# The loads of A and B move from SyncE's queue to ScalarE's, behind its copies of z

## The chip, the cores and the metric

The kernel runs on one core of a Trainium2 chip. The metric is the device time of one execution in microseconds. SyncE (SP) issues DMAs and waits; TensorE (PE), VectorE (DVE), ScalarE (ACT) and GpSimd (POOL) compute. ScalarE can issue DMAs too, on a queue of its own.

## The reference

For each of 64 batches `x[b]` (128 channels by 2048 times, f32) goes through two residual steps. The first picks one of 16 matrices of 128 x 128 by an id, the second one of 64 low rank adapters (A and B, rank 16) by another id:

```python
W = weights[itok_B_0_15]
x = x + jnp.einsum('bct,bcd->bdt', x, W)
Bx = jnp.einsum('bni,bri->bnr', x, B[itok_B_4_50])
x = x + jnp.einsum('bnr,bor->bno', Bx, A[itok_B_4_50])   # scaling 1
```

Each x is read once and each output written once, 1 MB (2^20 bytes) a batch each way. A and B of a batch lie side by side in one row of `lora`, 256 KB, which one DMA brings into `ab_in`.

## The kernel before

Two batches are a round, two kinds of round alternate, and two rounds (four batches, `BODY`) are a turn. Turn 0 and the last turn are written out, the 14 between them are a hardware loop on every engine. Buffers `x_in`, `x_out`, `ab_in`, `at`, `z_all`, `m_sel` have four copies each, one for each batch of a turn. PSUM's eight banks (`bank`) hold 512 columns each.

What happens to one batch:

- SyncE loads x (`load_x`, L128) and A with B (`load_ab`, L131). The id of the adapter is read from SBUF into a register (`value_load`, L125).
- GpSimd makes `m_sel`, the chosen matrix plus the identity (L209).
- TensorE mixes x by `m_sel` in four units of 512 columns (`mix_units`, L388). Each unit fills a bank. A round has only three banks for its eight units (`F_BANKS`), so from the fourth unit on TensorE waits until ScalarE has copied the unit three before it.
- ScalarE copies each unit from its bank to `ft` (`copy_units`, L256).
- TensorE multiplies `ft` by B (`sum_z`, L404) into a z bank, in four parts of 16 rows. ScalarE and VectorE copy two parts each out of it (`take_z`, L263 and L312).
- GpSimd adds the four parts in three additions (L218, L223) into the first 16 rows of `z_all`. ScalarE copies these rows to three other places (`place_z`, L268).
- VectorE transposes A (L328, semaphore `a_turned`). One round later TensorE multiplies it by z (`add_low_rank`, L428), and VectorE adds `ft` to it and writes `x_out` (L319). SyncE stores it (`store`, L149).

Each engine carries out its own list in the order written. In a round, TensorE mixes both batches, sums z of both, and then does the low rank product of the two batches of the round before. ScalarE copies eight units, takes z of both batches, places z of both. SyncE stores the two batches of a turn ago, loads two x as soon as the slots are free (`f_made`), and then loads A and B for the batches four further on. That last step (`next_ab`) waits until z of the slot's batch is made and A is transposed, since both read `ab_in`.

Instructions of VectorE, ScalarE and GpSimd are handed to the engine by its sequencer, which also does the register reads and arithmetic, the branches and the issuing of DMAs, in the order of the program.

Of the kernel before, what the change touches and what calls it, by code (L numbers as in the profile page):

```python
# [10 lines left out]
BATCHES, CHANNELS, TIME = 64, 128, 2048  # L11
# [15 lines left out]
ROUND = 2  # L27
BODY = 2 * ROUND
# [16 lines left out]
def live(count):  # L45

    return not (isinstance(count, int) and count <= 0)


def begun(b):  # L50

    return not (isinstance(b, int) and b < 0)


def f_bank_of(kind, k, u, final):

    return LAST_F[u] if final and k == ROUND - 1 else F_BANKS[kind][(UNITS * k + u) % len(F_BANKS[kind])]


def cond_lora_residual(nc, x, both_ids, weights, lora, out):  # L60
    with ExitStack() as ctx:
        def sbuf(name, shape, dtype=F32):
            return ctx.enter_context(nc.sbuf_tensor(name, shape, dtype))
# [4 lines left out]
        def sem(name):  # L68
            return ctx.enter_context(nc.semaphore(name))
# [3 lines left out]
        ids = sbuf("ids", [1, 2, BATCHES], I32)  # L73
# [6 lines left out]
        ab_in = [sbuf(f"ab_in{k}", [P, (JS + CHUNKS) * RANK]) for k in range(BODY)]  # L80
# [9 lines left out]
        ids_in = sem("ids_in")  # L90
# [3 lines left out]
        ab_loaded = [sem(f"ab_loaded{k}") for k in range(BODY)]  # L94
# [5 lines left out]
        a_turned = sem("a_turned")  # L100
# [3 lines left out]
        z_done = sem("z_done")  # L104
# [9 lines left out]
        def rows_of_unit(u):  # L114
            return slice(BLOCK * u, BLOCK * u + RANK)

        def rows_of_z(z_bank, c):
            return bank[z_bank][TILE * c:TILE * c + RANK, 0:P]
# [3 lines left out]
        @block.sync  # L122
        def _(sp):
            def adapter_of(b):
                return sp.value_load(ids[0:1, 1, bass.ds(b, 1)], min_val=0, max_val=lora.shape[0] - 1)  # L125

            def load_x(k, b):
                sp.dma_start(x_in[k][:], x[b]).then_inc(x_loaded[k], 16)  # L128

            def load_ab(k, adapter):  # L130
                sp.dma_start(ab_in[k][:], lora[adapter]).then_inc(ab_loaded[k], 16)  # L131

            sp.dma_start(ids[:].rearrange("p n b -> p (n b)"), both_ids).then_inc(ids_in, 16)  # L133
            sp.dma_start(w_all[:], weights).then_inc(w_in, 16)  # L134
            for i in range(2):
                cols = slice(TIME // 2 * i, TIME // 2 * (i + 1))
                sp.dma_start(x_in[0][:, cols], x[0, :, cols]).then_inc(first_loaded[i], 16)
            load_x(1, 1)
            sp.wait_ge(ids_in, 16)
            for k in range(ROUND):  # L140
                load_ab(k, adapter_of(k))
            for k in range(ROUND, BODY):
                load_x(k, k)
            for k in range(ROUND, BODY):
                load_ab(k, adapter_of(k))

            def store(k, b):
                sp.wait_ge(added, UNITS * (b + 1))
                sp.dma_start(out[b], x_out[k][:]).then_inc(stored[k], 16)  # L149

            def next_x(k, b):
                sp.wait_ge(f_made, UNITS * (b - BODY + 1))
                load_x(k, b)

            def next_ab(k, b):
                adapter = adapter_of(b)
                sp.wait_ge(z_done, b - BODY + 1)
                sp.wait_ge(a_turned, b - BODY + 1)
                load_ab(k, adapter)


            def turn(q, last):
                for kind in range(KINDS):
                    b = BODY * q + ROUND * kind
                    slots = range(ROUND * kind, ROUND * (kind + 1))
                    if begun(b - BODY):
                        for i, k in enumerate(slots):
                            store(k, b - BODY + i)
                    if not last:
                        for i, k in enumerate(slots):  # L170
                            next_x(k, b + BODY + i)
                        for i, k in enumerate(slots):
                            next_ab(k, b + BODY + i)

            turn(0, False)
            with sp.Fori(1, TURNS - 1) as q:
                turn(q, False)
            turn(TURNS - 1, True)

            def store_part(b, units):  # L180
                cols = slice(UNIT * units[0], UNIT * (units[-1] + 1))
                sp.dma_start(out[b, :, cols], x_out[b % BODY][:, cols]).then_inc(stored[b % BODY], 16)

            for k in range(BODY - 2):
                store(k, BATCHES - BODY + k)
            for units in ((0, 1), (2, 3)):
                sp.wait_ge(added, UNITS * (BATCHES - 2) + units[1] + 1)
                store_part(BATCHES - 2, units)
            sp.wait_ge(evacuated, 2)
            store_part(BATCHES - 1, (1, 2))  # L190
            sp.wait_ge(added, UNITS * (BATCHES - 1) + 1)
            store_part(BATCHES - 1, (0,))
            for k in range(BODY - 2):
                sp.wait_ge(stored[k], 16 * TURNS)
            sp.wait_ge(stored[BODY - 2], 16 * (TURNS - 1 + 2))
            sp.wait_ge(stored[BODY - 1], 16 * (TURNS - 1 + 3))
# [51 lines left out]
        @block.scalar  # L248
        def _(act):
            def copy_units(kind, i, b, final):  # L250
                k = ROUND * kind + i
                for u in range(UNITS):
                    if live(UNITS * (b - BODY) + u + 1):
                        act.wait_ge(added, UNITS * (b - BODY) + u + 1)
                    act.wait_ge(f_made, UNITS * b + u + 1)
                    nc.scalar.copy(ft[k][u][:], bank[f_bank_of(kind, i, u, final)][:]).then_inc(copied, 1)  # L256

            def take_z(i, b, z_bank):
                act.wait_ge(z_done, b + 1)
                if live(b - 1):  # L260
                    act.wait_ge(z_paired, 2 * (b - 1))
                for c in (0, 2):
                    nc.scalar.copy(z_part[i][c][:], rows_of_z(z_bank, c)).then_inc(z_taken_act, 1)  # L263

            def place_z(k, b):
                act.wait_ge(z_summed, b + 1)
                for u in range(1, UNITS):
                    nc.scalar.copy(z_all[k][rows_of_unit(u), :], z_all[k][rows_of_unit(0), :]).then_inc(z_placed, 1)  # L268

            def normal_round(kind, b):  # L270
                for i in range(ROUND):
                    copy_units(kind, i, b + i, False)
                for i in range(ROUND):
                    take_z(i, b + i, Z_BANKS[i])
                for i in range(ROUND):
                    place_z(ROUND * kind + i, b + i)

            def turn(q):
                for kind in range(KINDS):
                    normal_round(kind, BODY * q + ROUND * kind)  # L280

            turn(0)
            with act.Fori(1, TURNS - 1) as q:
                turn(q)
            normal_round(0, BATCHES - BODY)
            b = BATCHES - 2
            copy_units(1, 0, b, True)
            take_z(0, b, Z_BANKS[0])
            place_z(BODY - 2, b)
            b = BATCHES - 1  # L290
            copy_units(1, 1, b, True)
            take_z(1, b, Z_BANKS[0])
            act.wait_ge(z_summed, BATCHES)
            for u in BY_ACT:
                nc.scalar.copy(z_all[BODY - 1][rows_of_unit(u), :], z_all[BODY - 1][rows_of_unit(BY_DVE[0]), :]  # L295
                               ).then_inc(z_placed, 1)
            act.wait_ge(stored[BODY - 1], 16 * (TURNS - 1))
            act.wait_ge(low_done, BATCHES)
            for u in range(1, UNITS):
                nc.scalar.copy(x_out[BODY - 1][:, UNIT * u:UNIT * (u + 1)], bank[LAST_OWN[u]][:]).then_inc(evacuated, 1)  # L300
            act.wait_ge(evacuated, UNITS - 1)
            cols = slice(UNIT * (UNITS - 1), TIME)
            act.dma_start(out[BATCHES - 1, :, cols], x_out[BODY - 1][:, cols]).then_inc(stored[BODY - 1], 16)
# [200 lines left out]
```

## Time and profile before

| | |
|---|---|
| median of 3 runs | 393.79 us (390.11 to 395.64) |
| the profiled execution | 395.34 us, its span 393.5 us |
| granted TensorE clock, mean | 0.982 of full |
| busy: PE, PE weight loads, DVE, ACT, POOL | 376.5, 354.3, 230.8, 238.4, 112.2 us |
| DMA queue of SyncE | 151.79 MB, 96.1% of the 16 engines' span |
| issues: x, stores, A with B | x63, x62 of 1 MB, x64 of 256 KB (and the parts of the first x and the last stores) |

Times in rows are us from the start of the span, except where they say ns. The span goes from the first to the last instruction, and the execution's own time lies 1.8 us above it. Busy time of an engine doesn't count what its sequencer does: register reads, waits, branches and the issue of DMAs. Rows of a sequencer have a q behind the engine (SPq, ACTq). An f32 matmul shows as two records. In brackets stands the idle time of the engine before the row and who ended it.

### The profile page before, as it was taken

To read this page: it belongs to the slowest core of one execution; us is meant where nothing else is said; L and a number is where in the kernel's file an instruction comes from. 1 tells how busy PE (TensorE), PEld (TensorE's weight loads), DVE (VectorE), ACT (ScalarE), POOL (GpSimd) and SP (SyncE) were. 2 spreads that over 40 slices of the span, in tenths; PEclk is the share of its full clock that TensorE was granted. 3 is DMA by queue.
4 is the path that set the end of the run, shared out by engine and by line. 5 is a ranking of instruction groups with operands and counts; after the bars stand their busy time and mean duration, and the time that the engine had idled before them with its cause. 6 is when DMAs were issued, how large, how long until landed. Compare 5 with 4: busy or idle time off the path is not lost.

```text
span 393.5 us, 16869 instructions
## 1 busy us (share of the span) xinstructions
PE 376.5 (96%) x6170; PEld 354.3 (90%) x6170; DVE 230.8 (59%) x447; ACT 238.4 (61%) x579; POOL 112.2 (29%) x260
## 2 busy tenths in 40 slices
PE   7989989999999999999999999999999999999981
PEld 7979979999999999999999999999999999999871
DVE  0226762676555667755566775556677555667763
ACT  1566644666656666665666666566666666666541
POOL 2122330333332223333222333322233332223210
PEclk9999988999999999999999999999999999999996
DMA  7999997999999999999999999999999999999567
GB/s 272 417 362 347 407 409 277 345 415 386 406 414 412 408 416 415 415 404 414 404 418 410 416 405 410 414 405 409 414 415 414 410 406 406 415 403 413 223 250 277
DMA packets 28383, 152.24 MB, mean 387 GB/s; under 512 B 3153, under 2 KB 3154, under 8 KB 12242
## 3 DMA queue, kind: packets, MB, share of 16 engines
q1 hardware_dynamic: 28226, 151.79, 96.1%
q10 hardware_dynamic: 144, 0.26, 0.2%
q8 instruction: 9, 0.15, 0.1%
q14 instruction: 4, 0.03, 0.0%
HBM read 84.94 MB, written 67.11 MB: 386 GB/s over the span
## 4 chain that ended last, share of the span: by engine, by line
PE 93%; DMA 2%; issue 2%; ACT 1%; DVE 1%; POOL 1%; SPq 0%; POOLq 0%; DVEq 0%; ACTq 0%
PE bank L388 60%; PE bank L428 16%; PE bank L404 16%; DMA x_in<-in_x 2%; POOL z_pair L218 0%; ACT x_out L300 0%; DVE x_out L319 0%; ACT z_all L268 0%; POOL z_all L223 0%; ACT ft L256 0%; DVE z_pair L335 0%; DVE z_part L312 0%; DVE z_all L339 0%; SPq L134 0%; SPq L133 0%
## 5 line engine op out<-in xcount | busy, mean ns | idle before, releaser
L388 PE MATMUL bank<-m_sel,x_in 128*128 128x128 f32 x2048 | 240.8, 279 | 2.9 <-ACT ft L256 1.7
L388 PEld LDWEIGHTS bank<-m_sel,x_in 128*128 128x128 f32 x2048 | 234.1, 194 | 8.6 <-DVE x_out L319 2.7
L256 ACT COPY ft<-bank 128x512 f32<-128x512 f32 x256 | 146.1, 587 | 65.5 <-PE bank L388 63.5
L319 DVE TENSOR_TENSOR x_out<-bank,ft 128x512 f32<-128x512 f32 x253 | 154.3, 681 | 19.6 <-PE bank L428 19.5
L218 POOL TENSOR_TENSOR z_pair<-z_part 16x128 f32<-16x128 f32 x126 | 54.2, 446 | 217.0 <-DVE z_part L312 198.6
L312 DVE COPY z_part<-bank 16x128 f32<-16x128 f32 x126 | 36.2, 287 | 121.2 <-PE bank L404 119.2
L268 ACT COPY z_all<-z_all 16x128 f32<-16x128 f32 x189 | 56.0, 296 | 46.9 <-POOL z_all L223 43.8
L428 PE MATMUL bank<-z_all,at 16*128 16x128 f32 x2048 | 70.0, 282 | 2.8 <-issue 1.8
L428 PEld LDWEIGHTS bank<-z_all,at 16*128 16x128 f32 x2048 | 63.2, 187 | 10.1 <-issue 10.0
L404 PE MATMUL bank<-ft,ab_in 128*16 128x128 f32 x2048 | 65.6, 274 | 1.6 <-issue 1.6
L404 PEld LDWEIGHTS bank<-ft,ab_in 128*16 128x16 f32 x2048 | 51.4, 96 | 10.6 <-issue 5.1
L263 ACT COPY z_part<-bank 16x128 f32<-16x128 f32 x128 | 32.9, 257 | 33.2 <-PE bank L404 31.6
L328 DVE STREAM_TRANSPOSE at<-ab_in 128x512 f32<-128x512 f32 x64 | 41.5, 684 | 14.5 <-DMA ab_in<-in_lora 14.5
L209 POOL TENSOR_TENSOR m_sel<-w_all,ident 128x128 f32<-128x128 f32 x64 | 29.2, 457 | 38.9 <-PE bank L388 23.4
L223 POOL TENSOR_TENSOR z_all<-z_pair 16x128 f32<-16x128 f32 x63 | 28.1, 446 | 7.3 <-POOL z_pair L218 4.5
L436 PE MATMUL bank<-ident 128*128 128x128 f32 x26 | 5.9, 427 | 1.6 <-POOL ident L202 1.6
L436 PEld LDWEIGHTS bank<-ident 128*128 128x128 f32 x26 | 5.6, 331 | 1.6 <-POOL ident L202 1.6
L300 ACT COPY x_out<-bank 128x512 f32<-128x512 f32 x3 | 1.6, 594 | 1.5 <-PE bank L428 1.5
L256 ACT ACT_TABLE_LOAD x1 | 1.3, 1283 | 0.8 <-PEq L489 0.8
L295 ACT COPY z_all<-z_all 16x128 f32<-16x128 f32 x2 | 0.6, 295 | 0.8 <-DVE z_all L339 0.8
L335 DVE TENSOR_TENSOR z_pair<-bank,z_part 16x128 f32<-16x128 f32 x2 | 0.6, 287 | 0.8 <-ACT z_part L263 0.7
L339 DVE TENSOR_TENSOR z_all<-z_pair 16x128 f32<-16x128 f32 x2 | 0.6, 280 | 0.1
(7 smaller groups left out, 0.9 us busy)
## 6 DMA issues: line engine op xcount, KB each, us to landing
x_in<-in_x SPq DMA_DIRECT2D x63, 1024.0 KB, 11.3
out<-x_out SPq DMA_DIRECT2D x62, 1024.0 KB, 10.1
ab_in<-in_lora SPq DMA_DIRECT2D x64, 256.0 KB, 10.0
out<-x_out SPq DMA_DIRECT2D x3, 512.0 KB, 4.3
w_all<-in_weights SPq DMA_DIRECT2D x1, 1024.0 KB, 4.9
x_in<-in_x SPq DMA_DIRECT2D x2, 512.0 KB, 6.9
out<-x_out SPq DMA_DIRECT2D x1, 256.0 KB, 4.6
out<-x_out ACTq DMA_DIRECT2D x1, 256.0 KB, 5.9
```

What stands on the lines that cost most here:

```text
L209: nc.gpsimd.tensor_tensor(m_sel[k][:], w_all[:, cond, :], ident[:], ALU.add).then_inc(m_picked, 1)
L218: nc.gpsimd.tensor_tensor(z_pair[i][:], parts[2 * i][:], parts[2 * i + 1][:], ALU.add).then_inc(z_paired, 1)
L223: nc.gpsimd.tensor_tensor(z_all[k][rows_of_unit(0), :], z_pair[0][:], z_pair[1][:], ALU.add).then_inc(z_summed, 1)
L256: nc.scalar.copy(ft[k][u][:], bank[f_bank_of(kind, i, u, final)][:]).then_inc(copied, 1)
L263: nc.scalar.copy(z_part[i][c][:], rows_of_z(z_bank, c)).then_inc(z_taken_act, 1)
L268: nc.scalar.copy(z_all[k][rows_of_unit(u), :], z_all[k][rows_of_unit(0), :]).then_inc(z_placed, 1)
L312: nc.vector.tensor_copy(z_part[i][c][:], rows_of_z(z_bank, c)).then_inc(z_taken_dve, 1)
L319: nc.vector.tensor_tensor(x_out[k][:, UNIT * u:UNIT * (u + 1)], bank[banks[u]][:], ft[k][u][:], ALU.add).then_inc(added, 1)
L328: nc.vector.transpose(at[k][:], blocks).then_inc(a_turned, 1)
L388: last = nc.tensor.matmul(to[:, P * c:P * (c + 1)], x_in[k][:, UNIT * u + P * c:UNIT * u + P * (c + 1)], m_sel[k][:], start=(c == 0), stop ...
L404: last = nc.tensor.matmul(rows_of_z(z_bank, c), ab_in[k][:, first:first + RANK], ft[k][u][:, P * c:P * (c + 1)], start=(u == 0), stop=(u = ...
L428: last = nc.tensor.matmul(bank[banks[u]][:, P * c:P * (c + 1)], at[k][rows, js, :].rearrange("r j i -> r (j i)"), z_all[k][rows, :], start ...
```

## The change

SyncE's `next_ab` goes. ScalarE gets one of its own: it reads the adapter's id into a register, waits for `a_turned`, and issues the load. It runs in each normal round but the last, between the second `take_z` and the first `place_z`. The wait for `z_done` isn't repeated, for `take_z` has just waited for the same. The loads of the first four batches stay with SyncE. The semaphores that tell of a landed load are the same.

```diff
--- before.py
+++ after.py
@@ -152,12 +152,6 @@
                 sp.wait_ge(f_made, UNITS * (b - BODY + 1))
                 load_x(k, b)
 
-            def next_ab(k, b):
-                adapter = adapter_of(b)
-                sp.wait_ge(z_done, b - BODY + 1)
-                sp.wait_ge(a_turned, b - BODY + 1)
-                load_ab(k, adapter)
-
 
             def turn(q, last):
                 for kind in range(KINDS):
@@ -169,8 +163,6 @@
                     if not last:
                         for i, k in enumerate(slots):
                             next_x(k, b + BODY + i)
-                        for i, k in enumerate(slots):
-                            next_ab(k, b + BODY + i)
 
             turn(0, False)
             with sp.Fori(1, TURNS - 1) as q:
@@ -267,11 +259,19 @@
                 for u in range(1, UNITS):
                     nc.scalar.copy(z_all[k][rows_of_unit(u), :], z_all[k][rows_of_unit(0), :]).then_inc(z_placed, 1)
 
-            def normal_round(kind, b):
+            def next_ab(k, b):
+                adapter = act.value_load(ids[0:1, 1, bass.ds(b, 1)], min_val=0, max_val=lora.shape[0] - 1)
+                act.wait_ge(a_turned, b - BODY + 1)
+                act.dma_start(ab_in[k][:], lora[adapter]).then_inc(ab_loaded[k], 16)
+
+            def normal_round(kind, b, last=False):
                 for i in range(ROUND):
                     copy_units(kind, i, b + i, False)
                 for i in range(ROUND):
                     take_z(i, b + i, Z_BANKS[i])
+                if not last:
+                    for i in range(ROUND):
+                        next_ab(ROUND * kind + i, b + BODY + i)
                 for i in range(ROUND):
                     place_z(ROUND * kind + i, b + i)
 
@@ -279,10 +279,11 @@
                 for kind in range(KINDS):
                     normal_round(kind, BODY * q + ROUND * kind)
 
+            act.wait_ge(ids_in, 16)
             turn(0)
             with act.Fori(1, TURNS - 1) as q:
                 turn(q)
-            normal_round(0, BATCHES - BODY)
+            normal_round(0, BATCHES - BODY, last=True)
             b = BATCHES - 2
             copy_units(1, 0, b, True)
             take_z(0, b, Z_BANKS[0])
```

## Rows read from the trace of the kernel before

**Rows 1.** The page: busy times, the queue, the chain that ended last.

```profile
PE 376.5 (96%) x6170; PEld 354.3 (90%) x6170; DVE 230.8 (59%) x447; ACT 238.4 (61%) x579; POOL 112.2 (29%) x260
...
q1 hardware_dynamic: 28226, 151.79, 96.1%
...
PE 93%; DMA 2%; issue 2%; ACT 1%; DVE 1%; POOL 1%; SPq 0%; POOLq 0%; DVEq 0%; ACTq 0%
```

**Rows 2.** Timeline, even round: start us, us, engine, line, operation, tiles, count, idle before.

```profile
205.73 1.73 SPq L131 DMA_DIRECT2D ab_in<-in_lora  x2
...
206.09 0.54 ACT L263 COPY z_part<-bank 16x128 f32<-16x128 f32 x2 [0.48 <-PE bank L404]
...
207.96 7.41 PE L388 MATMUL bank<-m_sel,x_in 128*128 128x128 f32 x64
...
209.93 1.60 ACT L256 COPY ft<-bank 128x512 f32<-128x512 f32 x3
...
211.99 1.29 DVE L328 STREAM_TRANSPOSE at<-ab_in 128x512 f32<-128x512 f32 x2
```

**Rows 3.** Timeline, the next, odd round.

```profile
217.44 0.54 ACT L263 COPY z_part<-bank 16x128 f32<-16x128 f32 x2 [0.39 <-PE bank L404]
...
218.69 0.94 ACT L268 COPY z_all<-z_all 16x128 f32<-16x128 f32 x3 [0.72 <-POOL z_all L223]
...
219.41 5.85 PE L388 MATMUL bank<-m_sel,x_in 128*128 128x128 f32 x50
...
220.25 0.94 ACT L268 COPY z_all<-z_all 16x128 f32<-16x128 f32 x3 [0.62 <-POOL z_all L223]
...
221.22 1.76 ACT L256 COPY ft<-bank 128x512 f32<-128x512 f32 x3
```

**Rows 4.** Landing of the x loads (L128) issued in 80:100 and in 340:360.

```profile
DMA to landing us min/median/max: 7.7/7.7/7.8
...
DMA to landing us min/median/max: 17.2/17.6/17.8
```

**Rows 5.** Timeline of the last rounds.

```profile
368.31 3.65 PEld L388 LDWEIGHTS bank<-m_sel,x_in 128*128 128x128 f32 x32 [0.21 <-DMA x_in<-in_x]
...
372.90 0.81 PEld L404 LDWEIGHTS bank<-ft,ab_in 128*16 128x16 f32 x32 [0.94 <-issue]
```

**Rows 6.** Timeline of the first round.

```profile
21.55 1.56 ACT L256 COPY ft<-bank 128x512 f32<-128x512 f32 x3
22.19 1.97 PEld L388 LDWEIGHTS bank<-m_sel,x_in 128*128 128x128 f32 x17 [1.84 <-ACT ft L256]
```

**Rows 7.** Timeline, an early pair of ab issues on SyncE.

```profile
39.66 1.56 SPq L131 DMA_DIRECT2D ab_in<-in_lora  x2
```

**Rows 8.** The ab issues (L131), ns min/median/max.

```profile
L131 SPq DMA_DIRECT2D ab_in<-in_lora x64: 332/333/857, 4.2 to 355.8; - x64
```

**Rows 9.** Register reads, SyncE in 60:160 and 160:360, GpSimd in 60:240.

```profile
L125 SPq TENSOR_LOAD <-ids x17: 264/285/653, 67.1 to 158.8; - x17
...
L125 SPq TENSOR_LOAD <-ids x35: 262/545/794, 160.4 to 355.1; - x35
...
L208 POOLq TENSOR_LOAD <-ids x30: 283/290/413, 71.1 to 232.4; - x30
```

**Rows 10.** The one DMA that ScalarE issues (L303).

```profile
L303 ACTq DMA_DIRECT2D out<-x_out x1: 374/374/374, 387.1 to 387.1; - x1
```

**Rows 11.** The chain in order of time, 48 to 72 us.

```profile
52.94 1.76 issue
...
56.38 10.03 PE bank L388 x64
```

**Rows 12.** ScalarE's L261 between 216.9 and 217.7 us.

```profile
L261 ACTq ALU_OP  x1: 38/38/38, 217.4 to 217.4; - x1
```

**Rows 13.** Windows: us, busy us of each engine, granted clock, DMA share, GB/s.

```profile
55.20:61.90 6.70, 6.70 (x45) 6.48 (x41) 4.19 (x7) 1.46 (x4) 0.92 (x2) 0.50 0.96 393
...
370.00:386.00 16.00, 12.73 (x244) 11.27 (x242) 12.58 (x24) 7.53 (x20) 1.30 (x3) 1.00 0.68 275
```

## The prediction, made before the change was run

> **What bounds the kernel now.** I read the page first: TensorE is busy 96% of the span and the 16 DMA engines 96% too, ScalarE 61%, and the chain that ended last is 93% TensorE [rows 1]. So two resources are nearly full, and the first question is which one sets the pace. The timeline of two rounds answers it [rows 2, 3]. A round handles two batches. TensorE runs 64 records of the mix (L388), 64 of the z product (L404) and 64 of the low rank product (L428), one set behind the other. The mix starts at 207.96 and again at 219.41, so a round takes 11.45 us. TensorE sets the pace, and whatever holds it adds to the time.
>
> The DMA queue is the second limit, not yet in force. The loads of x issued around 90 us land 7.7 us after their issue, those around 350 us 17.6 us after it [rows 4]. The backlog thus grows by 9.9 us in 260 us, which are 22.7 rounds: 0.44 us a round. The transfers would need 11.9 us for the work of a round, against TensorE's 11.45. The four x buffers pay for it: only at 368.31 does the mix wait for x, for 0.21 us [rows 5], just before the end. The transfers cost nothing today.
>
> **ScalarE's order, and how late it already is.** In each round ScalarE copies eight banks to `ft`, takes z of both batches (L263), waits for GpSimd's sum, and places z of both (L268), 0.94 us each. Then come the copies of the next round. The mix holds three banks, so its fourth unit waits until the first unit was copied. Of the 64 matmul records of a round's mix, eight are one unit. They take 7.41 us, 0.116 each, so unit 3 starts 24 records, 2.78 us, behind the mix: at 210.74 in one round and at 222.19 in the next. The first copy of the round is done at 209.93 + 0.59 = 210.52 and 221.22 + 0.59 = 221.81 [rows 2, 3]. What TensorE needs between the end of a copy and its start shows in the first round, where it did wait: copy from 21.55 to 22.14, TensorE at 22.19, 0.05 us [rows 6]. So ScalarE is early by only 0.17 us in one kind of round and 0.33 us in the other. That is all the cover that anything put ahead of `place_z` has, beside ScalarE's own idle time there (0.72 and 0.62 us before the two placings, waiting for GpSimd).
>
> **The change, part by part.** *Removed from SyncE:* two reads of an adapter id, the wait for z and `a_turned`, and two issues a round. SyncE is on the chain with 0% [rows 1], so its time is free today and stays so. Worth 0.
>
> *Added to ScalarE's sequencer,* behind the second `take_z` and ahead of the first `place_z`: twice the register read of the id, its range check, the address arithmetic, the wait for `a_turned`, and the DMA issue. The wait is free: the transposes of these batches ran at 211.99 and are over at 213.28, before z at 217.44 [rows 2, 3]. The rest costs sequencer time, and ScalarE's copies can't be dispatched meanwhile, though ScalarE itself is idle. Its price is on SyncE today. From the start of one ab issue to the start of the next there lies one whole sequence. A pair takes 1.56 us in all at 39.66 [rows 7] and 1.73 us at 205.73 [rows 2]; less one issue of 0.33 us [rows 8] that is 1.23 and 1.40 us a sequence. The spread is the register read: 285 ns median from 60 to 160 us and 545 ns from 160 to 360 us on SyncE, 290 ns up to 240 us on GpSimd [rows 9]; it is long where the backlog is long. On ScalarE the wait for z drops out (an estimated 0.05 us), and the issue is 374 ns instead of 333, from the one that ScalarE has [rows 10]. So a sequence costs 1.22 us at the low end and 1.39 at the high end, two 2.44 and 2.78.
>
> *The path that follows.* Odd round: the last `take_z` starts at 217.44. Plus 2.44, plus 0.05 to the first dispatched copy (an estimate) is 219.93; GpSimd's sums were ready when the placings began, at 218.69 and 220.25 [rows 3], so the first placing doesn't wait for them any more and the second hardly. Six placing copies take 2 x 0.965 (220.25 to 221.22 is one set with its gaps): 221.86. First `ft` copy 0.59, signal 0.05: 222.50. TensorE wants it at 222.19, so it stalls 0.31 us. Even round: 206.09 + 2.49 + 1.93 + 0.64 = 211.15 against 210.74: 0.41 us. Mean 0.36 us; by the high price 0.34 more, 0.70 us. The later copies catch up, each 0.59 us against 0.89 us of a unit, so it is one stall a round. I take 0.42 us, near the low end, because a slower round of TensorE (11.87 us) lets the transfers nearly keep up (11.9), the backlog stays at the values of the first half, and with it the reads stay short.
>
> *How often.* 30 rounds issue loads (turns 0 to 14, two each). In the round that ends at 66 us the mix takes 10.03 us instead of 7.4 [rows 11], so its fourth unit comes late anyway: no stall there. In the first, where TensorE waits for the copy already [rows 6], the shift counts in full, 0.6. So 29 stalls: 29 x 0.42 = 12.2 us; bounds 29 x 0.36 = 10.4 and 29 x 0.70 = 20.3. With the shortest reads of [rows 9], 264 ns, the 10.4 would be 9 at the least.
>
> *The loads themselves* move to ScalarE's queue. They may overtake x and stores. That holds up x by at most the bytes of two ab loads, 0.52 MB, at 386 GB/s (151.79 MB in 393.5 us [rows 1]) 1.35 us; x had room until 368 us [rows 5]. They are issued about 1.2 us later than today (SyncE's pair starts at 205.73 [rows 2]; ScalarE's first issue would be at 206.09 + 1.22 - 0.37 = 206.94) but are needed two rounds later. Both are worth 0 as long as TensorE is the slower one. The Trainium skill (DMA: Bandwidth & Descriptors, Issuing engines are not separate DMA queues) says that DMAs of all issuers run on the same 16 engines and that issuing from several saves only sequencer time. By that rule nothing is gained here at all, since SyncE's time was free; the sum is the same.
>
> **The sum.** The profiled execution took 395.34 us with a span of 393.5, 1.55 us above the median of the three runs, 393.79. It becomes 407.5; on the median, 393.8 + 12.2 = 406.0 us. A difference of 2%, 7.9 us, is about what a measurement of this kernel can tell from none.
>
> **The rivals.**
> *A: the sequencer runs ahead, no change.* If ScalarE's sequencer only queued the second `take_z` and went on, the reads would start as soon as z of the first batch was taken, at 216.51 instead of 217.44. 222.50 less 0.93 is 221.57, before 222.19: no stall, and from there on x is bound by the transfers at the very end, where ab in front of it costs up to 1.35 us. Time 394 to 395. It decides where the two sequences end before 219.6. Against it: a sequencer instruction of the second `take_z` (L261) starts at 217.4, when z is done and not when the first was taken [rows 12]; the wait lies on the sequencer itself. Chance 0.10.
> *B: long reads.* If ScalarE's reads cost what they cost late in the run, 0.545 us [rows 9], instead of some 0.27, two cost 0.55 us more: stall 0.36 + 0.55 = 0.91, times 29 = 26 us, 420 us. For it: the long reads are half of what the trace has; against it: they belong to a backlog that this change holds down. The Trainium skill (DMA: Bandwidth & Descriptors, Latency and other measured facts) gives a floor of about 600 ns for a register load; by that figure the stall would be 1.0 us and the time about 423, an estimate. The trace doesn't agree: 262 ns is its shortest, 290 a median [rows 9]. The same price would come if the first read waited for ScalarE's two copies of `take_z` to end (0.54 us), which no row settles. Chance 0.10.
> *C: the clock.* At 52.94 TensorE idled for 1.76 us, and from 55 to 62 us it was granted half of its clock, 1.2 GHz [rows 11, 13]. Were stalls of 0.4 us enough for that, each would cost far more and the time pass 430. The idle time of 0.94 us at 372.90 [rows 5] was followed by no fall up to 386 us [rows 13]. Chance 0.02. The opposite, that this one episode is absent, gives back 2.7 us and stays within 2%.
>
> **How the numbers follow.** Forecast 0.78, A 0.10, B 0.10, C 0.02. The likeliest gives 406. The forecast's own bounds are 393.8 + 10.4 = 404 to 414, widened by the 3 us by which the runs differ; A lies below, B above. The range of 399 to 418 leaves out A and most of B and C. Slower by over 2% (beyond 401.7): the forecast nearly whole, B and C, 0.82. Within 2%: A and the forecast's thin end, 0.16. Faster: 0.02, since nothing on the chain gets shorter.
>
> **What the changed profile would show.** Rounds of 11.8 to 11.9 us instead of 11.45. TensorE waiting for ScalarE (L256) at L388 once a round, some 0.4 us, 12 us in all, where today the first round has the one such wait [rows 6]. ScalarE's waits before `z_all` for GpSimd gone or small and counted to the sequencer's own work, the first placing at 2.5 us behind the last `take_z` and not 1.25. Loads of x landing after 8 to 12 us all along. ab landing faster than x. Register reads on ScalarE of 0.27 to 0.4 us. The prediction is wrong if the first placing starts within 2.1 us of the last `take_z` (A), if reads are at 0.55 us (B), or if x landing times set TensorE's waits.

## The result, and the profile after

The changed kernel takes 400.81 us (median of 4 runs, 400.31 to 402.57), the kernel before 393.22 us beside it (4 runs). The ratio is 1.021, with a 95% interval of 1.016 to 1.027. The kernel is slower, clear of noise; whether by more than 2% these runs can't tell, for the interval holds 1.02. The forecast was 406.0 us, with a range of 399 to 418. The profiled execution took 400.31 us, its span 398.5 us.

The page of the changed kernel: busy times, the two queues, the chain by engine. They answer to [rows 1]; q10 is ScalarE's queue.

```profile
PE 381.2 (96%) x6170; PEld 354.4 (89%) x6170; DVE 230.7 (58%) x447; ACT 236.7 (59%) x580; POOL 112.2 (28%) x260
...
q1 hardware_dynamic: 19586, 136.06, 85.6%
q10 hardware_dynamic: 8784, 15.99, 10.5%
...
PE 78%; DVE 9%; issue 5%; ACT 4%; DMA 2%; ACTq 0%; DVEq 0%; SPq 0%
```

TensorE is "busy" 4.7 us more, with the same 6170 records. Its weight loads take the same time as before. The rise is waiting inside the mix, as the timeline shows. First an even, then an odd round of the changed kernel (columns as in [rows 2, 3]; lines are shifted: 389 was 388, 248 was 256, 260 was 268, 255 was 263):

```profile
207.92 0.54 ACT L255 COPY z_part<-bank 16x128 f32<-16x128 f32 x2 [0.48 <-PE bank L405]
208.72 1.49 ACTq L265 DMA_DIRECT2D ab_in<-in_lora  x2
...
209.78 7.76 PE L389 MATMUL bank<-m_sel,x_in 128*128 128x128 f32 x64
210.25 1.91 ACT L260 COPY z_all<-z_all 16x128 f32<-16x128 f32 x6 [1.79 <-issue]
...
212.18 1.56 ACT L248 COPY ft<-bank 128x512 f32<-128x512 f32 x3
212.81 4.54 PEld L389 LDWEIGHTS bank<-m_sel,x_in 128*128 128x128 f32 x40 [0.28 <-ACT ft L248]
...
219.61 0.54 ACT L255 COPY z_part<-bank 16x128 f32<-16x128 f32 x2 [0.38 <-PE bank L405]
220.41 1.48 ACTq L265 DMA_DIRECT2D ab_in<-in_lora  x2
...
221.94 1.91 ACT L260 COPY z_all<-z_all 16x128 f32<-16x128 f32 x6 [1.78 <-issue]
...
223.87 1.57 ACT L248 COPY ft<-bank 128x512 f32<-128x512 f32 x3
224.50 1.86 PEld L389 LDWEIGHTS bank<-m_sel,x_in 128*128 128x128 f32 x16 [0.17 <-ACT ft L248]
```

Follow ScalarE in the odd round. The last `take_z` starts at 219.61, the pair of issues ends at 221.89, and the placing starts at 221.94, 2.33 us behind `take_z`, where it was 1.25 [rows 3]. All six placing copies now run without a pause (x6), for GpSimd's sums lie ready; before, each three waited for theirs. The first copy of the round goes out at 223.87, is done at 224.45, and TensorE takes up its fourth unit at 224.50, 0.05 us later, as in [rows 6]. From the last `take_z` to that unit are 4.89 us, in the even round as well (212.81 less 207.92).

When TensorE gets there by itself can be read in the kernel before. These are the weight loads of the fourth unit there, in the rounds of [rows 2, 3]:

```profile
210.63 0.19 PEld L388 LDWEIGHTS bank<-m_sel,x_in 128*128 128x128 f32 x1
...
222.08 0.19 PEld L388 LDWEIGHTS bank<-m_sel,x_in 128*128 128x128 f32 x1
```

They start 2.67 us behind the mix, 4.54 and 4.64 us behind the last `take_z`. The prediction had 2.78, 4.65 and 4.75: it took 24/64 of the 7.41 us of the records, which last up to the end of the last matmul, and so found about the start of the unit's first matmul (210.74). But its weight load comes first, and that is what waits for the copy. So ScalarE was early by only 0.06 and 0.22 us before the change, not 0.17 and 0.33, and the changed kernel is late by 0.35 and 0.25 us, 0.30 in the mean. The mix shows the same: its 64 records take 7.76 us instead of 7.41 in the even round, and from its start to the z product are 7.70 us instead of 7.34.

The waits of the whole run, in us, times, longest; the register reads on ScalarE; and the landing of x loads issued in 80:100 and 340:360, as [rows 4]:

```profile
ACT z_all L260 <- issue: 52.1, 29, 1.9
...
PEld bank L389 <- ACT ft L248: 8.8, 28, 2.4
```

```profile
L263 ACTq TENSOR_LOAD <-ids x60: 273/279/482, 18.0 to 361.9; - x60
```

```profile
DMA to landing us min/median/max: 8.3/8.8/8.9
...
DMA to landing us min/median/max: 7.3/7.8/8.0
```

TensorE's weight loads wait for ScalarE's copy 28 times. In 29 of the 30 rounds behind an issue, as forecast, the fourth unit starts 0.05 us behind that copy's end. ScalarE's own wait is called "issue": it waits for its sequencer. The loads of x keep landing after 8 to 9 us, where before it grew to 17.6 [rows 4].

The sum over the span: the sixth round's mix starts at 68.66 and the 31st's at 362.66, so 25 rounds take 294.0 us, 11.76 each. Before they took 286.5 (70.47 to 357.01), 11.46 each. That is +7.5 us, all of it the 0.30 us a round. The profiled execution of before lies 2.1 us above the median, with its stretch at the half clock from 55 to 62 us [rows 11, 13]; the changed kernel has only 3.4 us at 1.2 GHz (23.9 to 27.3), and is 1.8 us ahead by the sixth round. It gains 0.7 us more at the end. The difference of the spans, 5.0 us, is therefore smaller than that of the medians, 7.6. The 3.4 us lie behind the longest wait for a copy, in the second round:

```profile
23.01 6.36 PE L389 MATMUL bank<-m_sel,x_in 128*128 128x128 f32 x40 [2.19 <-ACT ft L248]
```

In the kernel before, the weight loads of that round waited 1.84 us [rows 6], here 2.38. There the 40 records behind the wait took 4.73 us with no fall of the clock, here 6.36.

### The profile page after: what moved, and what is told of

The parts are those of the page before. It is cut to its first block, busy times and chain, and to the rows that moved or that the text cites. A ratio compares the mean times of both kernels' runs of the same rounds, so it can differ in the third digit from the quotient of the medians.

```text
span 398.5 us, 16812 instructions
## 1 busy us (share of the span) xinstructions
PE 381.2 (96%) x6170; PEld 354.4 (89%) x6170; DVE 230.7 (58%) x447; ACT 236.7 (59%) x580; POOL 112.2 (28%) x260
## 3 DMA queue, kind: packets, MB, share of 16 engines
q10 hardware_dynamic: 8784, 15.99, 10.5%
## 4 chain that ended last, share of the span: by engine, by line
PE 78%; DVE 9%; issue 5%; ACT 4%; DMA 2%; ACTq 0%; DVEq 0%; SPq 0%
PE bank L389 50%; PE bank L405 16%; PE bank L429 12%; DVE x_out L320 9%; ACT ft L248 3%; DMA x_in<-in_x 2%; ACT z_all L260 1%; ACT x_out L301 0%; ACT L248 0%; ACTq L265 0%; ACTq L263 0%; DVE z_pair L336 0%; DVEq L309 0%; ACT z_part L255 0%; DVE z_all L340 0%
## 5 line engine op out<-in xcount | busy, mean ns | idle before, releaser
L389 PE MATMUL bank<-m_sel,x_in 128*128 128x128 f32 x2048 | 246.9, 279 | 5.8 <-ACT ft L248 2.7
L248 ACT COPY ft<-bank 128x512 f32<-128x512 f32 x256 | 143.9, 590 | 50.9 <-PE bank L389 49.6
L429 PE MATMUL bank<-z_all,at 16*128 16x128 f32 x2048 | 69.0, 281 | 1.1 <-DVE z_all L340 1.1
L405 PEld LDWEIGHTS bank<-ft,ab_in 128*16 128x16 f32 x2048 | 51.4, 96 | 10.4 <-issue 5.0
```

The costliest lines, as they stand in the source:

```text
L389: last = nc.tensor.matmul(to[:, P * c:P * (c + 1)], x_in[k][:, UNIT * u + P * c:UNIT * u + P * (c + 1)], m_sel[k][:], start=(c == 0), stop ...
L405: last = nc.tensor.matmul(rows_of_z(z_bank, c), ab_in[k][:, first:first + RANK], ft[k][u][:, P * c:P * (c + 1)], start=(u == 0), stop=(u = ...
L429: last = nc.tensor.matmul(bank[banks[u]][:, P * c:P * (c + 1)], at[k][rows, js, :].rearrange("r j i -> r (j i)"), z_all[k][rows, :], start ...
```

## The experiments

The theory after the result: what costs time is how long ScalarE's sequencer is occupied between the last `take_z` and the first copy of the next round, beyond a cover of some 2.0 us: the 4.54 and 4.64 us of TensorE less 2.56 us for placing, first copy and signal, which the changed kernel gives as 4.89 less 2.33. The expectations below were written with the cover of the prediction, 2.1 us, and with 0.10 us "for the restart" of TensorE on top. That 0.10 us is the same error of the cover under another name: once there is a stall, both ways of counting give the same sum, but there is no price of its own. The main rival: the loads themselves, on a second queue, overtaking x and stores. Times are medians with the ratio to the kernel before, run on the same chip. The diffs are shortened: `...` and words stand for the rest of the code.

**The same time spent with no load moved.** SyncE keeps all its loads; ScalarE makes four register reads of no use.

```diff
 (before the change, ScalarE)
+    def spare_read(b):
+        act.value_load(ids[0:1, 1, bass.ds(b, 1)], min_val=0, max_val=lora.shape[0] - 1)
     for i in range(ROUND): take_z(i, b + i, Z_BANKS[i])
+    if not last:
+        for i in range(4): spare_read(b + i % ROUND)
     for i in range(ROUND): place_z(...)
```

> All loads stay on SyncE as before the change; ScalarE makes four register reads of no use where the changed kernel has its two sequences, 4 x 0.62 = 2.5 us against 2.28. Theory: placing 2.55 us behind the last take_z, stall of 0.43 us and 0.10 us for the restart, 0.53 us a round, 407 to 408. Rival (queue or DMA issue is the cause): 393. Landing of x: if the second queue made the transfers faster, x lands later here than in the changed kernel (above 9 us); if the slower round did, after 7 to 8 us here too.

400.51 us, ratio 1.022 (1.015 to 1.029): the time of the changed kernel. Timeline of the run with four reads, an even round:

```profile
207.41 0.54 ACT L263 COPY z_part<-bank 16x128 f32<-16x128 f32 x2 [0.48 <-PE bank L411]
...
209.28 7.77 PE L395 MATMUL bank<-m_sel,x_in 128*128 128x128 f32 x64
209.75 1.90 ACT L268 COPY z_all<-z_all 16x128 f32<-16x128 f32 x6 [1.81 <-issue]
...
212.32 4.54 PEld L395 LDWEIGHTS bank<-m_sel,x_in 128*128 128x128 f32 x40 [0.28 <-ACT ft L256]
```

Of the reads behind one another the first took 0.62 us with its range check, the others 0.53 to 0.54, so the placing started 2.34 us behind `take_z` and not 2.5: by chance the same delay as in the changed kernel. With the same delay come the same 7.77 us of the mix, the same wait of 0.28 us, the same 11.76 us a round. The queue on which A and B travel makes no difference to the time that these runs could show. It makes none to x either: its loads land after 7.8 us around 90 us and after 8.0 around 350 us. What keeps the backlog down is the slower round. The expected time of 407 was missed because the price of a read was, not the rule.

**One read more.** The changed kernel with a fifth step behind its two loads.

```diff
     if not last:
         for i in range(ROUND): next_ab(ROUND * kind + i, b + BODY + i)
+        spare_read(b)
```

> The changed kernel with one more register read of no use behind the two issues, 0.62 us. Theory: with the cover used up, all of it counts: 0.62 x 29 = 18 us more than the changed kernel, 419; the 0.10 us of restart doesn't grow. Rival (TensorE or the transfers have room for some of it): under 410.

418.5 us, ratio 1.064 (1.059 to 1.070). An odd round of this run:

```profile
204.78 0.54 ACT L255 COPY z_part<-bank 16x128 f32<-16x128 f32 x2 [0.38 <-PE bank L409]
...
207.72 1.90 ACT L260 COPY z_all<-z_all 16x128 f32<-16x128 f32 x6 [2.40 <-POOL z_all L215]
209.64 1.56 ACT L248 COPY ft<-bank 128x512 f32<-128x512 f32 x3
```

The placing is at 2.94 us, 0.61 later, and the rounds take 12.36 us, 0.60 longer. Past the cover all of it counts. (The idle time of 2.40 us is put down to GpSimd here, which had long been done; it is again the sequencer's.)

**One read less.** The run with the useless reads, three instead of four.

```diff
-        for i in range(4): spare_read(b + i % ROUND)
+        for i in range(3): spare_read(b + i % ROUND)
```

> As the run with four useless reads and all loads on SyncE, with three reads: placing 1.80 us behind the last take_z instead of 2.34. From the start of the last take_z to the mix's fourth unit ScalarE's path is that delay plus 2.58 us (4.90 less 2.32 in the changed kernel), TensorE's own is 4.65 and 4.75 us. Theory: 1.80 + 2.58 = 4.38 is under both, so nothing is late although the first placing is 0.55 us later than before: rounds of 11.46 us, 393. Rival (the cost grows with every read from the first): 0.5 to 0.75 of the 7 us of four reads are left, 397 and above.

395.06 us, ratio 1.006 (1.003 to 1.010): neither nothing nor most of it. The trace says why. Register reads and ScalarE's copies, first up to 136 us, then behind it:

```profile
L271 ACTq TENSOR_LOAD <-ids x18: 273/277/283, 68.6 to 127.0; - x18
...
L271 ACTq TENSOR_LOAD <-ids x58: 274/413/691, 137.4 to 359.4; - x58
```

```profile
125.73 0.54 ACT L263 COPY z_part<-bank 16x128 f32<-16x128 f32 x2 [0.39 <-PE bank L411]
127.54 1.94 ACT L268 COPY z_all<-z_all 16x128 f32<-16x128 f32 x6 [1.26 <-POOL z_all L223]
129.50 1.79 ACT L256 COPY ft<-bank 128x512 f32<-128x512 f32 x3
...
347.38 0.54 ACT L263 COPY z_part<-bank 16x128 f32<-16x128 f32 x2 [0.51 <-PE bank L411]
349.91 1.90 ACT L268 COPY z_all<-z_all 16x128 f32<-16x128 f32 x6 [1.99 <-issue]
```

With reads of 0.277 us the placing begins 1.81 us behind `take_z`, 0.56 later than before the change, and costs nothing: the rounds from 70 to 139 us take 11.44 to 11.49 us. So the cover is not the 1.25 us up to the first placing but reaches to the fourth unit, over 1.8 us. Then, with rounds of 11.45 us, the backlog of the transfers grows (x lands after 7.7 us around 90 us, 13.6 around 350), the reads grow to 0.4 us and more, the placing slips to 2.1 and at last 2.5 us, and the stalls begin: rounds of 11.44 to 12.04 us. The backlog stops at 13.9 us. One of these rounds tells the two covers apart:

```profile
185.42 7.49 PE L395 MATMUL bank<-m_sel,x_in 128*128 128x128 f32 x64
```

Its fourth unit starts 4.62 us behind the last `take_z` (183.55). By the prediction's 4.65 nothing would be late; by the 4.54 it is 0.08 us late, and the 64 records take 7.49 us instead of 7.41. (The profiled execution, 399.95 us, is the slowest of the twelve, and has 6.8 us at the half clock.)

**Only one of the two loads on ScalarE.**

```diff
-        for i in range(ROUND): next_ab(ROUND * kind + i, b + BODY + i)
+        next_ab(ROUND * kind, b + BODY)          # the second stays with SyncE, as before
```

> Of the two loads of a round the first is issued by ScalarE where the changed kernel has both, the second by SyncE as before the change. Theory: 1.18 us behind the last take_z, cover 1.23 us: no stall, rounds of 11.46 us, 393 within 0.5%. If the cost went by the number of loads and not by a cover, half of it would be left: 397.

391.98 us, ratio 0.998 (0.994 to 1.002). Half of the loads on ScalarE cost nothing; it isn't half of the loss. In the trace the rounds from 65 to 295 us take 11.44 to 11.49 us. Behind that they are longer (11.5 to 13.1 us), the mix waiting for VectorE's `x_out` and 3.4 us at the half clock among them; no fourth unit waits for a copy there.

**Both loads on ScalarE, one at each of its waits.**

```diff
     for i in range(ROUND):
-        next_ab(...)        # both, ahead of both placings
-    for i in range(ROUND):
-        place_z(...)
+        if not last: next_ab(ROUND * kind + i, b + BODY + i)
+        place_z(ROUND * kind + i, b + i)
```

> The first load stands behind the second take_z as in the changed kernel, the second between the placing of the first z and that of the second. A sequence is 1.14 us. Theory: the first is over 1.18 us behind the last take_z, where placing began at 1.23 us before the change; the second lies in the wait for GpSimd's second sum, 1.56 us from placing to placing. Nothing is late: rounds of 11.46 us, 393 within 0.5%. With rounds of that length and the loads on ScalarE's queue, x lands after 17 us near the end if the second queue does nothing for the transfers, after less if it does. Rival (any load on ScalarE's queue costs TensorE time): 396 and above.

391.76 us, ratio 0.997 (0.993 to 1.001). ScalarE in the first half of this run, and the landing of x in 80:100 and 340:360:

```profile
121.00 0.54 ACT L255 COPY z_part<-bank 16x128 f32<-16x128 f32 x2 [0.38 <-PE bank L404]
121.80 0.35 ACTq L265 DMA_DIRECT2D ab_in<-in_lora  x1
122.26 0.94 ACT L260 COPY z_all<-z_all 16x128 f32<-16x128 f32 x3 [0.71 <-POOL z_all L215]
123.02 0.34 ACTq L265 DMA_DIRECT2D ab_in<-in_lora  x1
123.80 0.94 ACT L260 COPY z_all<-z_all 16x128 f32<-16x128 f32 x3 [0.61 <-POOL z_all L215]
```

```profile
DMA to landing us min/median/max: 8.4/9.4/10.0
...
DMA to landing us min/median/max: 15.9/16.0/16.1
```

Both placings wait for GpSimd as before the change, 0.71 and 0.61 us. The second load has slipped into the wait between them. The loads of A and B are all on ScalarE's queue, and the loss is gone: the rival of the queue falls a second time. From 240 us on, reads of 0.65 us (median) bring small stalls back, and the mean round is 11.52 us. The backlog grows here, as before the change. The gain over the kernel before, 1.1 us, is not clear of nothing. The profiled execution has no stretch at the half clock within the rounds.

**Each load behind its own `take_z`.**

```diff
     for i in range(ROUND):
         take_z(i, b + i, Z_BANKS[i])
+        if not last: next_ab(ROUND * kind + i, b + BODY + i)
```

> Each load stands right behind the take_z of its own batch: the first sequence lies in the wait for z of the second batch, the second in the wait for GpSimd's sum. Theory: each sequence of 1.14 us finds idle time of 0.9 to 1.2 us, the second take_z comes 0.2 to 0.3 us later, the first placing 0.2 to 0.3 us later, the second placing hardly; rounds of 11.46 us, 393 within 0.5%. Rival (the cost is of the loads on ScalarE's queue wherever they stand): 401.

399.26 us, ratio 1.015 (1.011 to 1.019). This missed: there was a second reader of ScalarE's progress that I had not seen. The timeline:

```profile
228.07 0.35 ACTq L265 DMA_DIRECT2D ab_in<-in_lora  x1
228.61 0.54 ACT L255 COPY z_part<-bank 16x128 f32<-16x128 f32 x2 [1.11 <-POOL z_pair L210]
...
229.20 0.98 PEld L428 LDWEIGHTS bank<-z_all,at 16*128 16x128 f32 x32 [0.45 <-ACT z_part L255]
```

The second low rank product writes the banks of z, so TensorE waits until both z are taken (`taken` in `add_low_rank`). The second `take_z` comes 1.64 us behind the first (226.97) instead of 1.01, and TensorE stalls there: it idles 0.45 us between the two low rank products, which ran on without a pause before, and from the first of them (227.78) to the next mix (230.31) are 2.53 us instead of 2.07 (205.89 to 207.96 in the kernel before). The fourth unit is on time. Most rounds up to 200 us take 11.60 us, those behind 200 us 11.90 to 11.95, where the first read of a pair takes some 0.6 us instead of 0.28. The mean round is 11.80 us.

**Behind both placings.**

```diff
     for i in range(ROUND): place_z(ROUND * kind + i, b + i)
+    if not last:
+        for i in range(ROUND): next_ab(ROUND * kind + i, b + BODY + i)
```

> Both loads behind the placing of both z, ahead of the first copy of the next round, so with no wait for GpSimd beside them. Theory: the last placing starts 2.81 us behind the last take_z as before the change; 2.28 us of sequences later the first copy goes out at 5.18 us, is done and told at 5.82 us, against TensorE's 4.70: stall of 1.12 us and 0.10 for the restart, times 29 = 35 us, 428. Rival (what counts is only how long ScalarE's sequencer is busy, wherever): as the changed kernel, 401.

437.6 us, ratio 1.114 (1.107 to 1.121). An even round:

```profile
231.85 0.94 ACT L260 COPY z_all<-z_all 16x128 f32<-16x128 f32 x3 [0.70 <-POOL z_all L215]
232.63 1.51 ACTq L265 DMA_DIRECT2D ab_in<-in_lora  x2
234.34 1.56 ACT L248 COPY ft<-bank 128x512 f32<-128x512 f32 x3 [1.55 <-PE bank L389]
234.98 1.19 PEld L389 LDWEIGHTS bank<-m_sel,x_in 128*128 128x128 f32 x10 [1.38 <-ACT ft L248]
```

The same two sequences at another place cost nearly six times as much (44.4 us against 7.6). The weight load of the fourth unit idles 1.38 us in this round. The path is 6.00 us here (234.98 less 228.98) and 6.15 in the next round, not 5.82: the register work and the branch of ScalarE's sequencer, which ran under the placing copies, stand free behind the loads as well, 0.18 to 0.33 us. That was missing in what I expected. Less the cover the stalls are 1.46 and 1.51 us, and these rounds take 12.90 and 12.98 us. In one round, at 86 us, ScalarE waited for `a_turned` on top, the copy came 1.4 us later still, and TensorE's weight loads idled 2.8 us; behind it lie 3.4 us at the half clock (92.1 to 95.5).

**The reads alone, early.** Both loads behind `take_z`, their reads between the last copies, where ScalarE idles 0.31 us for each unit.

```diff
     copy_units(kind, 1, b + 1, False, range(0, 2))
+    adapters = [read_id(b + BODY)]
     copy_units(kind, 1, b + 1, False, range(2, 3))
+    adapters.append(read_id(b + BODY + 1))
     copy_units(kind, 1, b + 1, False, range(3, 4))
     ... take_z, take_z, then wait for a_turned and issue, twice
```

> The same loads on ScalarE's queue, but their two register reads stand ahead of the copies of the last two units, where ScalarE waits for TensorE; only the wait and the two issues, some 0.5 us each, are left behind take_z. Theory (sequencer time ahead of place_z, past its cover): placing starts no later than before the change, rounds of 11.46 us, time 393 within 0.5%. Rival (loads on a second queue, overtaking x and stores, cost the time): as in the changed kernel, 401. Also open: whether loads of x land after 17 us near the end as before the change (the second queue does nothing for the transfers) or after less.

426.31 us, ratio 1.085 (1.081 to 1.090). A miss, by 33 us on the theory and by 25 on the rival. All reads of this run, and a round of it:

```profile
L263 ACTq TENSOR_LOAD <-ids x60: 276/894/1395, 14.3 to 382.4; - x60
```

```profile
228.12 0.59 ACT L248 COPY ft<-bank 128x512 f32<-128x512 f32 x1 [0.31 <-PE bank L398]
229.50 0.59 ACT L248 COPY ft<-bank 128x512 f32<-128x512 f32 x1 [0.80 <-PE bank L398]
...
231.22 0.59 ACT L248 COPY ft<-bank 128x512 f32<-128x512 f32 x1 [1.13 <-issue]
...
232.05 1.07 PE L414 MATMUL bank<-ft,ab_in 128*16 128x128 f32 x32 [1.19 <-ACT z_part L255]
```

The placing was on time, but a read took about 0.9 us and the next 1.2 instead of 0.28. The last copies came late, and TensorE waited for them in the z product, 1.3 us a round (rounds of 12.74). The theory was only half a theory as long as the price of a read was unknown. Loads of x landed after 6.8 us around 90 us and 6.7 around 350, less than in the kernel before, so it isn't the backlog. Two explanations are left: ScalarE's running copy of 128 x 512 holds the read up, or whatever else the chip does at that moment of the round.

**Reads at that moment on another engine, and on ScalarE at another moment.** In the first, SyncE makes four useless reads behind its first load of x in each round, in the changed kernel; in the second, ScalarE makes one behind the copies of the first batch, in the kernel before.

```diff
 (SyncE)                                    (ScalarE)
     next_x(k, b + BODY + i)                     copy_units(kind, i, b + i, False)
+    if i == 0: four value_loads            +    if i == 0: spare_read(b)
```

> The changed kernel, with four register reads of no use on SyncE behind the first load of x of each round, 5.3 to 7.7 us behind the start of the mix, where the reads on ScalarE took 0.9 and 1.2 us when they stood among its copies. If reads are slow there whoever makes them (the transfers of that moment), these take 0.6 us and more; if it is ScalarE's own copy of 128 x 512 that holds them up, they take 0.27 to 0.4. Time as of the changed kernel, 401, since SyncE waits there anyway.

> The kernel before the change with one register read of no use on ScalarE, behind the copies of the first batch, so that it starts while a copy of 128 x 512 runs, with other transfers under way than in the run with both reads early. If the copy holds the read up: 0.9 us or near it, in all rounds. If the transfers do: 0.28 to 0.8, changing along the run as on SyncE before the change. Time: the read with its checks takes up to 1.25 us where 0.89 us are free; ScalarE is then 0.36 us late for one copy, TensorE works three units ahead and doesn't wait: 393.

The first, a single run: 401.23 us; the second 392.99 us, ratio 0.999 (0.994 to 1.004). The reads:

```profile
L158 SPq TENSOR_LOAD <-ids x120: 261/796/1456, 13.0 to 359.3; - x120
```

```profile
L271 ACTq TENSOR_LOAD <-ids x31: 285/528/1188, 12.6 to 360.0; - x31
```

SyncE has no copies, and its reads at that moment take 0.8 us at the median and up to 1.46. In most rounds of the first half the first two, 5.7 and 6.9 us behind the start of the mix, take some 0.88 and 1.1 to 1.5 us, near the figures of ScalarE in the run before. So it isn't ScalarE's sequencer, held up by its own copy. ScalarE's read beside another copy takes 0.51 to 1.19 us from the third round on: 0.87 us in most rounds of the first half, 0.52 in most of the second. The copy is the same in both, so it doesn't set the price alone. Where they stood in the changed kernel, 10 to 11 us behind the start of the mix, reads took 0.28. What else goes on at the moment decides. That it is the transfers is likely but argued, not shown: the copies of the other engines at that moment were not taken away, and which transfers it would be (loads, stores, their write side) was not separated. It stays open.

The first of these runs shows one thing more. From 240 us on its loads of x land later, after 13.0 us around 350, and ScalarE's own reads, at their place in the changed kernel, rise from 0.278 us (median up to 260 us) to 0.396.

## Why the prediction was right, step by step

*What bounds the kernel, and the cover.* Right in kind. TensorE sets the pace, and the copy that frees the fourth unit's bank was just in time. The stalls are at that unit (8.8 us in 28 waits). The 0.05 us from the end of a copy to TensorE's start held in every stalled round. The cover was 0.11 us too long: 4.65 and 4.75 us instead of 4.54 and 4.64, because the unit's start was reckoned as a share of the mix, while the weight load that waits comes earlier.

*The price of the sequences.* Right in kind, too high in size. I had 1.22 to 1.39 us for one and 2.49 us for two with their dispatch. The issues on ScalarE are 1.14 us apart (1.49 us for the pair less an issue of 0.35) and the placing starts at 2.33. The difference is 0.16 us, 0.08 for each: an issue costs 0.347 us, not 0.374, and what fell away beside SyncE's sequence, the wait for z above all, was worth 0.10 us, not 0.05 (1.23 less 1.14, and the issue is 0.014 longer).

*The stall.* Forecast at 0.42 us a round with a low bound of 0.36; measured 0.30 us (0.35 and 0.25). This is the term that was mis-sized, by three errors: the path is 4.89 us, not 5.06 (0.17 too much), nothing is left of my surcharge of 0.06 for longer reads, for their median was 0.279 us over the whole run, and against these the cover was 0.11 too long. The 0.30 us times 29 rounds are 8.7 us, instead of 12.2.

The measured difference is 7.6 us. That is under the sum's own bounds, 10.4, or 9 with the shortest reads; 400.81 us lies in the range through the room that was added to them. And even 8.7 agrees with 7.6 in part by luck. In the changed kernel's trace the second round alone is 2.2 us longer than before (15.3 us, 13.2), 1.6 of it the half clock, which the sum left out. In the trace of before, the fourth and fifth rounds, with the idle 1.76 us and the half clock of [rows 11, 13], take 28.3 us; in the changed kernel's trace they take 23.6, without either. How often that stretch comes in the runs of before, whose times go from 390.11 to 395.64 us, one trace can't tell, and so the median of before carries an unknown part of it.

*The loads on their new queue, worth 0.* Shown: the same delay without a moved load gives the same time (400.5 us), and both loads at harmless places give the time of before (391.8 us).

*The transfers need 11.9 us for a round.* Wrong. With rounds of 11.76 us the landing of x doesn't grow, with the loads of A and B on either queue, so they need no more than that here. The forecast didn't hang on it, since it only asked that they not be the slower side.

*Rival A* (the sequencer runs ahead) is ruled out: the first issue starts 0.80 us behind the start of the last `take_z`, which is a whole sequence of 1.14 less the issue itself. *Rival B* (reads of 0.55 us) did not come about in this kernel, and the ground that I gave, the backlog, holds for this place in the round: with x landing after 8 us the reads stayed at 0.279 us, and where it lands after 13 to 16 us (three reads, one load at each wait, the useless reads on SyncE) reads at the same place took 0.40 to 0.65 us at the median. But it was only half the ground. With reads at an earlier moment of the round they took 0.9 and 1.2 us although x landed after 6.8 us, and the time was 426. That the change puts its reads at a quiet moment was luck. *Rival C* (the clock) is ruled out for the small stalls: the granted clock is 1.00 from 68 to 374 us. It did fall once, behind the wait of the second round (2.38 us of the weight loads), and cost 1.6 us there. In the run with useless reads on SyncE it didn't, behind a wait of 2.37 us.

## What to carry to other kernels

Before work is put on a sequencer "where the engine waits anyway", follow its chain to the next place where the bounding engine needs it, and take that as the cover: here 2.0 us although the wait filled was only 1.25, and at the places a few instructions earlier and later it was far less. Read the moment of that need from a record of its own, not from a share of a longer stretch: here that was 0.11 us wrong, at a loss of 0.30. List every reader of that engine's progress, not only the nearest. Put small steps one at a time into separate waits (391.8 us) rather than in one block (400.8 us), and ask whether the idle engine can keep them.

## What the runs showed of the hardware that was not expected

- A register read from SBUF takes 0.26 to 0.30 us in a quiet moment and up to 1.46 us in another part of the same round, on SyncE as on ScalarE. It goes with the moment in the round, and at one and the same place with how far the transfers are behind: 0.277 us at x landings around 8 us, 0.413 at 13.6 (medians, three reads). What holds it up was not shown.
- A bank must be free for the first weight load of its unit, not for its first matmul, here 0.11 us earlier (210.63 and 210.74). Without a wait this load runs under the matmul before it. Behind a wait it stands free, so from the unit's first matmul to the z product are 4.66 us instead of 4.56, whether the wait was 0.2 us or 0.8; from its first weight load they are 4.67 and 4.67. A stall reckoned from the matmuls alone comes out 0.10 us too small.
- The backlog of the transfers is no simple sum. At 11.76 us a round it stood still at 8 us in two kernels; at 11.45 it grew from 7.7 to 17.6. With each load behind its own `take_z` it grew from 8.4 to 11.6 us at a mean round of 11.80, but that mean hides two stretches, 11.60 us in most rounds up to 200 us and 11.90 and more behind it, and the landing rose mainly at the end of the first, from 8.1 us at 141 us to 10.5 at 211. In the changed kernel with useless reads on SyncE, which issue the second x of a round later, it stood at 8 us up to 215 us and then rose to 13 in rounds of 11.68 us and more. Why, was not tried.
